# Layer 0 of a two-layer block: three of four row groups are normalised by ScalarE instead of VectorE

## What is computed

```
x = x + tanh(g_xattn[0]) * xattn(layernorm(x), ctx, ctx)     # softmax over 77 keys
y = layernorm(x)                                             # (x - mean) / sqrt(var + eps)
x = x + tanh(g_ffn[0]) * ffn(y)
# ffn begins with:  scale = max(max(abs(y)) / 32767, 1e-12)
#                   y = clip(round(y / scale), -32768, 32767) * scale
#                   up = y @ w_up.T ;  gate = y @ w_gate.T ; ...
```

## Time and profile before

| | us |
|---|---|
| three runs | 511.07, 512.28, 517.63 |
| their median | 512.28 |
| the profiled execution, whole | 510.01 |
| its span (first to last instruction) | 508.0 |
| PE busy in it | 420.0 (83%) |
| DVE busy | 334.9 (66%) |
| ACT busy | 256.6 (51%) |
| POOL busy | 115.8 (23%) |

### The profile page before, as it was taken

How to read it: one execution, slowest core, us unless ns; L and a number is a source line. 1 busy time by engine, 2 the same in 40 slices (tenths; PEclk the granted TensorE clock), 3 DMA queues, 4 the chain that set the end, 5 groups by cost and what they waited for, 6 DMA issues and landing times.

```text
span 508.0 us, 7274 instructions
## 1 busy us (share of the span) xinstructions
PE 420.0 (83%) x2132; PEld 283.8 (56%) x2133; DVE 334.9 (66%) x739; ACT 256.6 (51%) x446; POOL 115.8 (23%) x135
## 2 busy tenths in 40 slices
PE   5995699999973008999999999999882699999992
PEld 4784444444432007888676677666651357676771
DVE  3689874359996999545567676667857254545551
ACT  2472655479985858014465556655641334242310
POOL 5431146000000000300590000100100734543122
PEclk9996799999997557999999999999995599999998
DMA  7900000000010031000793000000034312121000
GB/s 224 258 1 0 1 3 0 0 0 0 0 55 0 0 76 26 1 1 1 280 395 152 1 1 1 1 0 2 1 104 146 87 49 67 59 57 45 14 30 0
DMA packets 27387, 27.16 MB, mean 53 GB/s; under 512 B 11580, under 2 KB 23555, under 8 KB 27108
## 3 DMA queue, kind: packets, MB, share of 16 engines
q1 hardware_dynamic: 25155, 21.73, 13.3%
q0 software_dynamic: 2208, 5.14, 3.4%
HBM read 22.63 MB, written 5.15 MB: 55 GB/s over the span
## 4 chain that ended last, share of the span: by engine, by line
PE 66%; DVE 10%; ACT 6%; issue 5%; POOL 1%; DMA 1%; DVEq 0%; ACTq 0%; POOLq 0%
PE bank L1528 55%; PE bank L1776 5%; PE bank L1575 2%; ACT big_u L728 2%; PE bank L1969 2%; PE bank L1794 1%; ACT tmp L842 1%; DVE big_g L1249 1%; DVE mx L1344 1%; ACT tmp L838 1%; DVE big_g L1345 1%; DVE amP L1253 1%; PE bank L1802 1%; DMA big_u<-token_rows,k_blockdiag 1%; DVE tmp L1460 0%
## 5 line engine op out<-in xcount | busy, mean ns | idle before, releaser
L1528 PE MATMUL bank<-yT,ffn_w 128*128 x192 | 84.4, 602 | 4.0 <-ACT yT L728 2.8
L728 ACT ACTIVATE big_u<-bank 77x512 f32<-77x512 f32 (+3 forms) x102 | 56.2, 581 | 25.7 <-PE bank L1776 24.3
L1528 PEld LDWEIGHTS bank<-yT,ffn_w 128*128 128x128 f32 x192 | 36.9, 193 | 50.3 <-issue 48.1
L1528 PE MATMUL bank<-ffn_w,big_u 128*128 128x256 f32 x192 | 44.6, 393 | 6.9 <-ACT big_u L728 6.9
L1528 PEld LDWEIGHTS bank<-ffn_w,big_u 128*128 128x128 f32 x192 | 37.7, 198 | 12.4 <-ACT big_u L728 7.0
L1528 PE MATMUL bank<-big_g,yT 128*128 x92 | 43.7, 619 | 0.7 <-issue 0.7
L1528 PE MATMUL bank<-big_u,yT 128*128 x184 | 41.8, 380 | 1.6 <-DVE yT L1491 1.6
L977 ACT ACTIVATE yT<-yT 128x512 f32<-128x512 f32 x23 | 14.5, 630 | 56.3 <-DVE yT L1487 53.8
L901 ACT ACTIVATE big_g<-big_g 128x308 f32<-128x308 f32 x64 | 29.0, 457 | 26.0 <-DVE big_g L1345 25.5
L1528 PE MATMUL bank<-k_blockdiag,big_g 128*128 128x308 f32 x128 | 40.1, 429 | 2.4 <-DVE big_g L1345 2.2
L728 ACT ACTIVATE yT<-bank 128x256 f32<-128x256 f32 (+1 forms) x51 | 21.2, 465 | 39.4 <-PE bank L1575 26.5
(11 more groups left out here) (267 smaller groups left out, 789.4 us busy)
## 6 DMA issues: line engine op xcount, KB each, us to landing
big_g<-in_L_ffn_W SPq DMA_DIRECT2D x1, 4096.0 KB, 13.5
big_u<-in_L_ffn_W SPq DMA_DIRECT2D x1, 4096.0 KB, 25.1
x_rows<-in_x SPq DMA_DIRECT2D x2, 1024.0 KB, 7.8
ffn_w<-in_L_ffn_b SPq DMA_DIRECT2D x1, 2048.0 KB, 26.0
tmp<-bias_by_distance SPq DMA_DIRECT2D x2, 616.0 KB, 5.7
token_rows<-x_rows SPq DMA_DIRECT2D x1, 1032.0 KB, 6.7
tmp<-in_L_ffn_b SPq DMA_DIRECT2D x1, 1024.0 KB, 5.1
token_rows<-x_rows SPq DMA_DIRECT2D x1, 774.0 KB, 9.0
```

The costliest lines, as they stand in the source:

```text
L728: act.activation(out_, in_, ACT.Copy, **k).then_inc(done, 1)
L1528: return pe.matmul(out_, lhsT=lhsT, rhs=rhs, start=first, stop=last)
```

## The change

ACT now makes y for the groups 0, 1 and 2, one instruction for each tile: scale times x plus a shift. POOL makes the shift, minus mean times factor, with one small multiplication ahead of the two old instructions and one behind them; the semaphore that tells that a group's factor is ready moves to the last of the four. Group 3 is still made by DVE, from mean and factor. DVE takes the largest value of each group of ACT one step later than before: behind the attention of the next group. A new semaphore largest_y tells that this is done, so that `y2a` may be written again. PE turns group 0 one round later (g == 2), and group 1 behind attended0(3).

```diff
@@ POOL
             for g in range(NT // 4):
-                rstds(4 * g, s.mv_b, s.rstd_b, 2)
+                pool.wait_ge(s.mv_b, 4 * g + 4)
+                if g:
+                    pool.wait_ge(s.y_b, 4 * g)
+                pool.tensor_scalar(shift[:, :], mv[:, :, 0], -1.0, None, ALU.mult)
+                c.link(pool.tensor_scalar(ve[:, :], mv[:, :, 1], EPS, None, ALU.add))
+                c.link(pool.tensor_tensor(rstd[:, :], ve[:, :], mhalf[:, 0:4], ALU.pow))
+                pool.tensor_tensor(shift[:, :], shift[:, :], rstd[:, :], ALU.mult).then_inc(s.rstd_b, 1)
                 if g == 0:
                     pool.wait_ge(s.y_b, 4)
                     quantised(0, 1)
@@ ACT
+            def normalised(g):
+                act.wait_ge(s.rstd_b, g + 1)
+                if g:
+                    act.wait_ge(s.y2T_ps, CH * g)
+                    act.wait_ge(s.largest_y, g)
+                for u in range(4):
+                    act.activation(y2a[:, u, :], X[:, 4 * g + u, 0:D], ACT.Identity, scale=rstd[:, u:u + 1],
+                                   bias=shift[:, u:u + 1]).then_inc(s.y_b, 1)
...
                 if g == 1:
+                    normalised(0)
+                if g == 2:
                     y2T_out(0)
+                    normalised(1)
             y2T_out(1)
+            normalised(2)
             y2T_out(2)
@@ DVE
             def y2_largest(g):
                 dve.wait_ge(s.y_b, 4 * g + 4)
-                c.mark(dve.tensor_reduce(amY[:, g:g + 1], y2a, AX.XY, ALU.max, apply_absolute_value=True))
+                dve.tensor_reduce(amY[:, g:g + 1], y2a, AX.XY, ALU.max,
+                                  apply_absolute_value=True).then_inc(s.largest_y, 1)
...
             def stats_b(g):
+                if g:
+                    dve.wait_ge(s.rstd_b, g)
                 stats([X[:, 4 * g + u, 0:D] for u in range(4)], s.mv_b, (s.x1_done, 4 * g + 4))
 
-            for g in range(2):
-                attended(g)
-                stats_b(g)
-                scores0(g + 2)
-                y2_made(g)
-                y2_largest(g)
+            attended(0)
+            stats_b(0)
+            scores0(2)
+            attended(1)
+            y2_largest(0)
+            stats_b(1)
+            scores0(3)
             attended(2)
+            y2_largest(1)
             stats_b(2)
             attended(3)
-            y2_made(2)
+            y2_largest(2)
             stats_b(3)
-            y2_largest(2)
-            dve.wait_ge(s.dve_step, c.base + c.n)
+            dve.wait_ge(s.largest_y, 3)
             y2_made(3)
             y2_largest(3)
@@ PE
                 attended0(g)
                 if g < 2:
                     x_in(g + 2)
-                if g == 1:
+                if g == 2:
                     y2_in(0)
             weights0T(3)
+            attended0(3)
             y2_in(1)
-            attended0(3)
             y2_in(2)
```

More of the change, by code:

```diff
@@ L132, in __init__ @@
         self.y_b = sem("y_b")
+        self.largest_y = sem("largest_y")
         self.y2T_ps = sem("y2T_ps")
@@ L327, in flamingo_kernel @@
         rstd = sb("rstd", [P, 4])
+        shift = sb("shift", [P, 4])
         nmax = sb("nmax", [P, 4])
@@ L1125, in step_of @@
                     scalar(k + 1, sc[:, k + 1:k + 2], ALU.mult, unit)
-            dve.wait_ge(s.dve_step, c.base + c.n)
+            dve.wait_ge(s.largest_y, NT // 4)
             c.link(dve.tensor_reduce(sc[:, 0:1], amY[:, :], AX.X, ALU.max))
```

## The result

| | before | changed |
|---|---|---|
| median of 20 runs, us | 511.89 | 517.60 |
| lowest to highest | 510.06 to 517.63 | 516.39 to 521.55 |
| ratio, 95% interval | | 1.0125 (1.0107 to 1.0142) |
| span of the profiled execution | 508.0 | 515.1 |

By the ratio the change costs 1.25%, some 6.4 us of 511.9; the two medians differ by 5.7 us (1.1%), still inside the interval. That is within 2% and clear of the noise of 20 runs. A slow run is left out of a ratio, as one of the five of the kernel "PE filled" is (520.84 us).

What follows compares the result with a forecast made beforehand. VectorE was taken as the bound up to the last y2_largest; normalised(2) at 53.2 to 54.6 plus 7.9 gave 6.1 us later, 516.1 profiled, plus 1.3 for a typical run: 517.4. The 8-in-10 range was 513.0 to 521.5.

Steps and rivals of the forecast that it cites:

- the stage's loss: From group 2's nmax to the last y2_largest: ends 5.1 to 6.5 us later, taken as 6.1.
- The price of one group on ScalarE: Normalising one group on ScalarE: 3 x 0.50 + 0.59 = 2.1 us, against 1.38 on VectorE.
- The three waits: VectorE ahead of y2_largest for groups 0, 1, 2, waiting for ScalarE: about 2.7, 2.6 and 3 to 4 us.
- the two ends of my range: End of the last y2_largest: 5.1 us later with PE at the upper clock level, 6.5 at the lower.
- step 5: Behind normalised(2): y2_largest(2) 1.2, stats_b(3) 1.9, POOL 2.15, y2_made(3) to the end 2.63; sum 7.9, less 0.1 overlap.
- The shift goes through to the end: Behind the quantisation's scale: same work in the same order, so the 6.1 us reach the program's end.
- The rival that the clock makes it worse: PE thinner from 43 to 66 us, ffn products at the lower clock: 520 to 524 us; chance 0.10 (0.05 over 2%).
- The argument against it: PE's clock: before, y2_in(1) and the turning of weights alone restored the upper level within 50 to 56 us.
- The distance from there to a typical run: Whole program: typical run put 1.3 us above the profiled execution, between 1.1 (lowest run) and 2.3 (median).
- VectorE's own ledger: VectorE: new ScalarE waits 2.7 + 2.6 + 3.3, POOL wait 2.15 where 0.54 was, less 4.1 saved, is 6.1 us.
- The rival that VectorE doesn't wait: VectorE's stretch: ScalarE always ends its group ahead of y2_largest; 2.7 us earlier, 507.3 profiled; chance 0.05.
- the loss is taken back later: In the ffn: a wait ended by something else absorbs part of 6 us, giving 510 to 513; chance 0.07.

Runs made afterwards that it cites:

- PE filled: Changed kernel with 86 turnings of the identity into an unread bank in four pauses of PE: 1.0051 of the kernel before, median 513.52 us.
- doubled pass: Changed kernel with ScalarE computing each of groups 0 to 2 twice, first into an unused place: 1.0241 of the kernel before, 12.3 us above.
- order-alone kernel: Changed kernel with VectorE making y of all groups, new order and POOL's shift kept: 1.0031 of the kernel before.
- two buffers: Changed kernel with a second y buffer, y2_largest one step later, normalised(1) and POOL's weight block moved, no group 3 shift: 0.9925 of before, median 508.11 us.
- its 36: Kernel with two buffers plus 36 turnings of the identity into an unread bank on PE: 0.9874 of the kernel before, median 505.73 us.

## Why the prediction was right

Median predicted 517.4, measured 517.6; the stage's loss predicted as 6.1 us, measured as 6.10.

- **The price of one group on ScalarE**, taken from the form near the program's end, was 2.1 us; it is 2.06. One instruction took 0.589 us. The estimate of 0.51 us, worked out from the budget of the Trainium skill (ScalarE: Activation LUTs, Rules for kernel authors), was too low here, as the row had said.
- **The three waits** were forecast at 2.7, 2.6 and 3 to 4; they are 2.69, 2.69 and 3.41. The doubled pass and the order-alone kernel show that ScalarE's queue makes them. Into the third goes PE too: with PE filled it is 2.41, and there POOL's factor holds ScalarE.
- **nmax of group 3** came at 41.38, forecast 41.3; **attended0(3)** started at 46.36, forecast 46.4, and took 3.78 at the lower clock, forecast 3.62. Filling PE took it to 1.99 and gave 1.4 us of the stage back; the two ends of my range, at the two levels, were 5.1 and 6.5, and the filled kernel's stage is 4.7 above before, so the lower end was 0.4 too high.
- **POOL**: 2.15 forecast, 2.12 measured; the part of its two small instructions 0.5 forecast, 0.58 measured.
- **y2_largest(2) no longer beside POOL's work** was in the sum as part of step 5, and putting it back gave 3.04 us. That is more than the 1.2 us of y2_largest(2), because the statistics of group 3 (1.9 us) then lie in the wait for ScalarE as well. The sum had both terms and was right in total, but the prediction named only the first as a cost of the order.

What was off: the clock. I had y2_in(1) partly at the upper level; it ran at the lower one, and so did all of PE's work until 70. "The shift goes through to the end" left out 0.31 us at the diag product and 0.26 at the ffn's first products. The rival that the clock makes it worse was thus true in kind, with some 0.6 us in place of the 4 it needed. The argument against it did not hold: the row at 49.94 that it takes for y2_in(1) is y2_in(2), and after the change the same pair, y2_in(2) and the turning of weights, ran from 54.49 to 59.02 without bringing the upper level back. Why it came back before and not here stays open. The turning of weights took 2.77 us in place of 2.00, and ScalarE's copies behind it ended at 59.66, not by 58; that cost nothing.

That the median came out within 0.2 us is in part luck. For the profiled execution the prediction had 516.1, and it took 517.3: 1.2 short. The distance from there to a typical run had been put at 1.3, and was 0.3. The two errors cancel. The rise over the median before, 5.1 in the prediction (517.4 less 512.28), was 5.7, or 6.4 by the ratio. "VectorE's own ledger" reached 6.1 with two small terms missing that also cancel: a wait for POOL of 0.28 us before y2_made(1), which went away, and one for PE of 0.29 in attended(3), which came. And two per cent is not what a measurement of this kernel tells from no change: the interval here is 0.2% to either side.

The rival that VectorE doesn't wait was wrong for this kernel but right as a possibility: its sum was 2.7 us under before (its terms add up to 2.6), and the kernel with two buffers gave 3.6 in the stage. It had put POOL's step at its full 2.15 behind stats_b(3), with y2_largest(2) ahead of it, where two buffers had them side by side and the step, without the shift, at 1.6. That the loss is taken back later was shown false by the kernels without filling: what the stage lost or won arrived in the time (1.25 and 1.6 us for the order alone, 12.0 and 12.3 for the doubled pass, 3.1 and 2.8 with y2_largest(2) moved, 3.6 and 3.8 won with two buffers).

## What to carry to other kernels

An engine with idle time is not free where its idle time is a wait for the same chain. Before moving work, walk its queue and ask when it reaches the moved instruction and what now stands behind it. Here a reader one step behind its producer, with a single buffer, wasn't enough; a second buffer, one more step of distance and POOL's shift left out for the last group, taken together, turned 6.1 us lost into 3.6 won with the same normalisations on the same engines. Two waits that were side by side shouldn't be put one behind the other: look at what each long handover had beside it.

## What the runs showed of the hardware

In the changed kernel PE's clock fell at 42.8 us, within weights0T(3), behind a pause of 1.5 us and ahead of the one of 2.9 us. It then stayed at 1.2 GHz for 27 us, in which PE worked in pieces of 5.5, 4.5 and 2.6 us with pauses of 2.64, 2.07 and 2.84 us behind them. The moment of the fall is not fixed by the kernel. The changed kernel, the one with y2_largest(2) moved and the one without the shift for group 3 give PE the same work up to there, but the clock fell 10.3, 13.0 and 5.4 us behind the end of nmax of group 2, and it came back at different times. So in a single profile a part of PE's times, attended0(3) above all, is that execution's. 86 idle turnings kept the clock at 2.4 GHz throughout the stretch, and cost nothing that shows: the turnings end before the real work is ready, and the stage with two buffers is 20.0 us with and without its 36.

An instruction of ScalarE with scale and bias from memory on 128x256 takes 0.586 to 0.589 us and four in a row 2.06; VectorE's subtract and multiply of the same tiles takes 1.38. Nothing in these runs shows them disturbing each other: VectorE's normalisations, statistics and maxima are as long as before in every kernel.
